# Attention and gated experts on one core: row sums of the probabilities on VectorE, values' products in four array tiles, rounding of the second input on ScalarE and GpSimd

## What is computed

```python
x = x + attn(layernorm(x))         # softmax over 64 keys, then p @ v, then @ Wo.T
p = jax.nn.softmax(scores, axis=-1)
out = jnp.einsum('bhnqk,bhnkd->bhnqd', p, v2)
h = layernorm(x)                    # the second input
y = combine * (silu(h @ w_gate) * (h @ w_up)) @ w_down, summed over experts
x = x + y + shared(h)
```

## Time and profile before

| | |
|---|---|
| median of three runs | 735.25 us (733.56 to 737.29) |
| the profiled execution | 735.13 us, its span 733.3 us |
| TensorE | 690.8 us busy (94%) |
| TensorE weight load | 565.5 us (77%) |
| VectorE | 523.7 us (71%) |
| ScalarE | 532.6 us (73%) |
| GpSimd | 453.3 us (62%) |
| granted TensorE clock | 0.991 of full speed |

### The profile page before, as it was taken

How to read it: one execution, slowest core, us unless ns; L and a number is a source line. 1 busy time by engine, 2 the same in 40 slices (tenths; PEclk the granted TensorE clock), 3 DMA queues, 4 the chain that set the end, 5 groups by cost and what they waited for, 6 DMA issues and landing times.

```text
span 733.3 us, 19496 instructions
## 1 busy us (share of the span) xinstructions
PE 690.8 (94%) x6296; PEld 565.5 (77%) x6296; DVE 523.7 (71%) x1620; ACT 532.6 (73%) x1603; POOL 453.3 (62%) x561
## 2 busy tenths in 40 slices
PE   3899789999999999999999999999999999999997
PEld 2778668787887878788787878788787878778775
DVE  2466676868677786968677786867778686977664
ACT  3686868788787878787787868777787878764332
POOL 6233156767777676767777686777767586445433
PEclk9999999999999999999999999999999999999999
DMA  5010032140413123040314123040313213041321
GB/s 169 1 30 29 2 89 73 37 136 8 131 42 116 57 82 91 24 122 27 119 55 116 57 67 106 11 134 29 116 57 102 71 49 111 4 130 32 116 75 43
DMA packets 50244, 52.59 MB, mean 72 GB/s; under 512 B 5664, under 2 KB 31904, under 8 KB 50080
## 3 DMA queue, kind: packets, MB, share of 16 engines
q1 hardware_dynamic: 50208, 52.14, 23.6%
HBM read 43.20 MB, written 4.72 MB: 65 GB/s over the span
## 4 chain that ended last, share of the span: by engine, by line
PE 65%; POOL 9%; issue 8%; ACT 8%; DVE 8%; DMA 1%; POOLq 0%; SPq 0%; DVEq 0%; ACTq 0%
PE PS L1015 10%; PE PS L822 9%; PE PS L860 9%; PE PS L947 8%; PE PS L824 8%; PE PS L823 8%; ACT probs L581 4%; PE PS L848 3%; POOL X L524 2%; DVE neg_max L738 2%; POOL hh L467 2%; POOL X L518 2%; POOL gate L462 2%; PE PS L1012 2%; PE PS L977 2%
## 5 line engine op out<-in xcount | busy, mean ns | idle before, releaser
L581 ACT ACTIVATE probs<-PS,neg_max 128x96 f32<-128x96 f32 (+1 forms) x1024 | 246.4, 349 | 87.2 <-DVE neg_max L738 87.2
L462 POOL TENSOR_TENSOR gate<-gate,spread 128x512 f32<-128x512 f32 x124 | 158.2, 1276 | 150.8 <-ACT gate L533 86.8
L730 DVE SCALAR_TENSOR_TENSOR tu<-th,PS 128x512 f32<-128x512 f32 x128 | 87.1, 680 | 88.7 <-ACT th L549 75.7
L1015 PE MATMUL PS<-wd,hh 128*128 128x128 f32 x1024 | 136.3, 276 | 4.8 <-DVE hh L791 2.4
L738 DVE TENSOR_REDUCE neg_max<-PS 128x4 f32<-128x384 f32 (+1 forms) x256 | 122.1, 516 | 20.5 <-PE PS L860 17.6
L1015 PEld LDWEIGHTS PS<-wd,hh 128*128 128x128 f32 x1024 | 126.7, 192 | 12.5 <-DVE hh L791 4.9
L467 POOL TENSOR_TENSOR hh<-gate,tu 128x512 f32<-128x512 f32 x100 | 128.2, 1282 | 7.8
L822 PE MATMUL PS<-x_hi,w_hi 128*128 128x512 f32 x288 | 124.6, 433 | 0.2 <-DVE tu L730 0.2
L716 DVE STREAM_TRANSPOSE probsT<-probs 128x768 f32<-128x768 f32 (+1 forms) x128 | 114.6, 895 | 0.0
L824 PE MATMUL PS<-x_lo,w_hi 128*128 128x512 f32 x288 | 114.2, 397 | 0.0
L823 PE MATMUL PS<-x_hi,w_lo 128*128 128x512 f32 x288 | 113.4, 394 | 0.0
(11 more groups left out here) (105 smaller groups left out, 954.4 us busy)
## 6 DMA issues: line engine op xcount, KB each, us to landing
spread<-weights_by_expert SPq DMA_DIRECT2D x248, 128.0 KB, 3.0
X<-x SPq DMA_DIRECT2D x32, 256.0 KB, 3.6
OUT<-H SPq DMA_DIRECT2D x16, 256.0 KB, 3.1
out<-OUT SPq DMA_DIRECT2D x16, 256.0 KB, 2.6
ffn_stage<-w_gu SPq DMA_DIRECT2D x1, 1152.0 KB, 5.6
wd<-w_down SPq DMA_DIRECT2D x1, 512.0 KB, 6.7
weights_by_expert<-cT SPq DMA_DIRECT2D x16, 32.0 KB, 1.6
probsT<-w_att SPq DMA_DIRECT2D x1, 192.0 KB, 3.0
```

The costliest lines, as they stand in the source:

```text
L462: tt(gate2[:, :], gate[:, k % 2, :], spread[:, k % SP_BUFS, :], ALU.mult).then_inc(s_g2, 1)
L581: ins = nc.scalar.activation(probs[:, u % 2, tt, 2 * rows + e, j0:KW], PS[:, rows, n * KW + j0:n * KW + KW], ACT.Exp, bias=neg_max[:, rows ...
L730: v_.scalar_tensor_tensor(tu[:, k % 2, :], th[:, :], 1.0, PS[:, 5, :], ALU.add, ALU.mult).then_inc(s_tu, 1)
L1015: ins = mm(PS[:, 7, r], hh[:, k % 2, r], wd[:, k, :], start=(k == 0 and n == 0), stop=(k == NP - 1), skip_group_check=True)
```

## The change

- The columns of ones go. `v_bd` has 32 columns per block, a product of L947 uses 32 columns of the array, and the four of a block of keys go to four sets of 32 partitions of the same 256 columns.
- VectorE adds up each unit's probabilities (`sum_probs`) into `sums` at the end of the steps that `SUMS` names, one or two units a step, and turns the 32x32 blocks of a sequence into `sums_t` after its fourth unit. In OT, TensorE transposes two halves and spreads `sums_t` over the tokens by four products of 32 columns with columns of the identity.
- `probs` has four buffers; ScalarE waits for the sum of four units ago, in place of the turning of two units ago.
- `x2_hi` is written by ScalarE from PSUM right behind `x2_f`; `x2_lo` by GpSimd at the end of the step, behind LN1. TensorE waits for `second_low_ready` and `second_input_copied` where it waited for the shared bank's semaphores.

```diff
 OE = 13
+SUMS = (11, 12, 13, 13, 14, 14, 15, 16)
 OT, ON, OW = 14, 15, 16
...
+PROB_BUFS = 4
...
 assert len({use[:2] for use in USES}) == len(USES)
-SPLIT = ((LATE, XT), (LATE, XT2), (LATE, XT2 + 4))
+SPLIT = ((LATE, XT),)
...
-ORDER_PER_SLOT = 7
+ORDER_PER_SLOT = 5
...
         v_keys = sb("v_keys", [P, NSB, HG, D])
-        v_bd = sb("v_bd", [P, 2, NSB, HG, 2, 32])
+        v_bd = sb("v_bd", [P, 2, NSB, HG, 32])
         neg_max = sb("neg_max", [P, 2, HG])
-        probs = sb("probs", [P, 2, 2, HG, KW])
+        probs = sb("probs", [P, PROB_BUFS, 2, HG, KW])
         probsT = sb("probsT", [P, 2, HG, NQ, 3, Q])
-        o_f = sb("o_f", [P, 2, T])
+        sums = sb("sums", [P, GB, Q])
+        sums_t = sb("sums_t", [P, GB, Q])
+        o_f = sb("o_f", [P, T])
         o_rs = sb("o_rs", [P, 8, 4])
...
-        headcol = const("headcol")
+        sums_of = ident.rearrange("p (v h c a) -> p c h a v", v=4, h=2, c=4)
...
-        s_ones = sem("ones_beside_values")
...
+        s_x2f = sem("second_input_copied")
+        s_x2l = sem("second_low_ready")
...
+        s_sum = sem("sums_ready")
+        s_sum_t = sem("sums_turned")
...
                         tt(keyrow[:, :], grouprow[:, 0:2], grouprow[:, 2:4], ALU.add).then_inc(s_pool, 1)
-                        for par in range(2):
-                            ones = headcol.unsqueeze(1).broadcast_to([P, NSB * HG, 32])
-                            tt(v_bd[:, par, :, :, 1, :].rearrange("p n g f -> p (n g) f"), ones, ones,
-                               ALU.mult).then_inc(s_ones, 1)
                     g, k = at(sl, s, FF, 1, NP)
...
                            ALU.mult).then_inc(s_xn1, 1)
+                    g, b = at(sl, s, XT2, 4, GB)
+                    if g:
+                        cols = slice(T * b, T * b + T)
+                        taken(pool, sl, s, LATE)
+                        tt(x2_lo[:, g.par, cols], x2_f[:, cols], x2_hi[:, g.par, cols].bitcast(F32),
+                           ALU.subtract).then_inc(s_x2l, 1)
...
                         side, bank = filled(act, sl, s, LATE)
-                        copy(x2_f[:, T * b:T * b + T], bank[:, 0:T]).then_inc(s_high[side], 1)
+                        copy(x2_f[:, T * b:T * b + T], bank[:, 0:T]).then_inc(s_x2f, 1)
+                        copy(x2_hi[:, g.par, T * b:T * b + T], bank[:, 0:T]).then_inc(s_taken[side], 1)
                     def between_halves():
...
                     g, u = at(sl, s, SC, 1, NU)
-                    if g and (u >= 2 or not (g.fixed and g.n == 0)):
-                        act.wait_ge(s_pt, g.n * NU + u - 1)
+                    if g and (u >= PROB_BUFS or not (g.fixed and g.n == 0)):
+                        act.wait_ge(s_sum, g.n * NU + u - PROB_BUFS + 1)
                     for rows in range(2):
...
                                 ins = nc.scalar.activation(
-                                    probs[:, u % 2, tt, 2 * rows + e, j0:KW], PS[:, rows, n * KW + j0:n * KW + KW],
+                                    probs[:, u % PROB_BUFS, tt, 2 * rows + e, j0:KW], PS[:, rows, n * KW + j0:n * KW + KW],
                                     ACT.Exp, bias=neg_max[:, rows, n:n + 1])
...
                         act.wait_ge(s_o_ps, g.n * GB + b + 1)
-                        copy(o_f[:, :, :], PS[:, 2, :].rearrange("p (j q) -> p j q", j=2)).then_inc(s_o, 1)
+                        copy(o_f[:, :], PS[:, 2, 0:T]).then_inc(s_o, 1)
                     g, _ = at(sl, s, XT)
...
                         for v in (2 * half, 2 * half + 1):
-                            ins = copy(v_bd[:, g.par, :, :, 0, D * v:D * v + D].rearrange("p n g d -> p (n g) d"),
+                            ins = copy(v_bd[:, g.par, :, :, D * v:D * v + D].rearrange("p n g d -> p (n g) d"),
                                        v_keys[:, :, :, :].rearrange("p n g d -> p (n g) d"), scale=grouprow[:, v:v + 1])
...
                             v_.transpose(probsT[:, b, :, t0:t0 + 2, c0:3, :].rearrange("p g t c q -> p t g (c q)"),
-                                         probs[:, u % 2, :, :, c0 * Q:KW]).then_inc(s_pt, 1)
+                                         probs[:, u % PROB_BUFS, :, :, c0 * Q:KW]).then_inc(s_pt, 1)
+
+                    def sum_probs():
+                        for u, stage in enumerate(SUMS):
+                            g, _ = at(sl, s, stage)
+                            if not g:
+                                continue
+                            b, t0 = u // 4, 2 * (u % 4)
+                            j0 = Q if u % 4 == 0 else 0
+                            v_.tensor_reduce(sums[:, b, HG * t0:HG * t0 + 2 * HG],
+                                             probs[:, u % PROB_BUFS, :, :, j0:KW].rearrange("p t g k -> p (t g) k"),
+                                             AX_X, ALU.add).then_inc(s_sum, 1)
+                            if u % 4 == 3:
+                                dve.wait_ge(s_sum, g.n * NU + u + 1)
+                                v_.transpose(sums_t[:, b, :], sums[:, b, :]).then_inc(s_sum_t, 1)
...
-                        o_t = bank.rearrange("p (a k v d) -> p a k v d", k=2, v=4, d=D)
-                        link(sl, v_.reciprocal(o_rs[:, :, :], o_t[:, :, 1, :, 0]))
+                        link(sl, v_.reciprocal(o_rs[:, :, :], bank[:, T:T + Q].rearrange("p (a v) -> p a v", v=4)))
                         v_.tensor_tensor(o_n[:, :, :].rearrange("p n (a v d) -> p (n a) v d", v=4, d=D),
-                                         o_t[:, :, 0, :, :],
+                                         bank[:, 0:T].rearrange("p (a v d) -> p a v d", v=4, d=D),
                                          o_rs[:, :, :].unsqueeze(3).broadcast_to([P, 8, 4, D]),
...
                     turn_probs()
-                    g, b = at(sl, s, XT2, 4, GB)
-                    if g:
-                        side, bank = high_out(sl, s, LATE)
-                        cols = slice(T * b, T * b + T)
-                        link(sl, v_.tensor_copy(x2_hi[:, g.par, cols], x2_f[:, cols]))
-                        split_low(x2_lo[:, g.par, cols], x2_f[:, cols], x2_hi[:, g.par, cols]).then_inc(s_taken[side], 1)
                     g, _ = at(sl, s, LN1)
...
                         ins.then_inc(s_taken[side], 1)
+                    sum_probs()
                     g, _ = at(sl, s, XT)
...
                         side, bank = free(EARLY)
-                        use = shared_use(slot_before(sl), (XT2 + 4) % STEPS, LATE)
-                        pe.wait_ge(s_high[use.bank], use.high + 1)
+                        pe.wait_ge(s_x2f, g.n * GB + GB)
                         if g.fixed and g.n == 0:
...
                         if turn_ == 0:
-                            if g.fixed and g.n == 0:
-                                pe.wait_ge(s_ones, 2)
                             pe.wait_ge(s_vb, g.n + 1)
...
                                 pt = probsT[:, b, a, :, :, :].rearrange("p t c q -> p (t c) q")
-                                r0, c0 = 64 * (a % 2), T * (a // 2) + Q * kb
-                                ins = mm(PS[r0:r0 + 64, 2, c0:c0 + Q * nq],
-                                         v_bd[:, g.par, b * NQ + kb, a, :, :].rearrange("p k f -> p (k f)"),
+                                ins = mm(PS[32 * a:32 * a + 32, 2, Q * kb:Q * kb + Q * nq],
+                                         v_bd[:, g.par, b * NQ + kb, a, :],
                                          pt[:, 3 * kb + 2:3 * kb + 2 + 2 * nq - 1:2, :],
-                                         start=(kb == 0 and a < 2), stop=(kb == NQ - 1), skip_group_check=True)
+                                         start=(kb == 0), stop=(kb == NQ - 1), skip_group_check=True)
                         if later:
...
                         pe.wait_ge(s_o, g.n * GB + b + 1)
-                        for n in range(4):
-                            half, j = divmod(n, 2)
-                            ins = nc.tensor.transpose(bank[:, P * n:P * n + P], o_f[:, j, P * half:P * half + P], ident)
+                        for half in range(2):
+                            nc.tensor.transpose(bank[:, P * half:P * half + P], o_f[:, P * half:P * half + P], ident)
+                        pe.wait_ge(s_sum_t, g.n * GB + b + 1)
+                        for c in range(4):
+                            ins = mm(PS[32 * c:32 * c + 32, RING[side], T:T + Q], sums_t[:, b, :], sums_of[:, c, :, :, :],
+                                     start=True, stop=True)
                         ins.then_inc(s_filled[side], 1)
...
                         x2 = x2_hi[:, g.par, :], x2_lo[:, g.par, :]
-                        taken(pe, slot_before(sl), (XT2 + 4) % STEPS, LATE)
+                        pe.wait_ge(s_x2l, g.n * GB + GB)
                         for place, n in ((POST, WG), (LATE, WU)):
```

## The result

The changed kernel takes 729.5 us (median, 729.06 to 729.94) against 737.1 for the kernel before (733.56 to 737.96). The ratio of the fast runs is 0.9928, 95% interval 0.9904 to 0.9951; the two medians alone would give 0.990. The profiled execution took 729.39 us, its span 727.6 against 733.3.

What follows compares the result with a forecast made beforehand. It saw a relay between engines, TensorE only seemingly the bound; 0.1 + 0.6 + 0.2 + 0.3 = 1.2 us a slot over 12.5 slots gives 15, filling some 1: 16 off 735.1, 719 us; forecast 712 to 725, range 706 to 735.

Steps and rivals of the forecast that it cites:

- rival 1: Sums in the way: sums of 1.1 us instead of 0.9 lose some 0.6 a slot on VectorE, 727 us; chance 18%.
- Product stages, -2.5 us of TensorE: TensorE's product stages: four tiles at once instead of two save 2.5 us a slot, at best 2.73, at worst 0.
- Rival 2: Still two tiles at a time: product stages stay at 1.48 and 1.25 us, 734 us likeliest; chance 13%.
- OT stage, +0.1 each: TensorE's OT stage: two transposes go, four tiny products come; +0.1 us a stage, 0.2 a slot.
- Sums, 0.90 and 0.62 us: VectorE's eight sums a slot: 0.90 us for each of 768 elements, 0.62 for each of 512.
- rival 3: Slower: sums blocked by GpSimd, stalling 0.65 us each, five of them without room, 753 us; chance 9%.
- Steps 1 to 3, -0.1: VectorE gets a 0.62 us sum and loses 0.63 of rounding; 0.1 less a slot because the scores come earlier.
- Step 4, -0.6: Normalising chain: statistics of X end 0.62 us further ahead of tu, so GpSimd starts sooner; 0.6 us less.
- Step 5, -0.2: Two sums and a small transpose fit on VectorE, 6.3 us against 6.70; ScalarE's smaller o_f copy saves 0.2.
- Step 6, nothing: VectorE gets sums of 0.62 and 0.90 us, about 4.6 us against 4.85: no change.
- Step 7, -0.3: ScalarE gets some 0.3 us of rounding, TensorE's earlier transposes save most of its 0.54 us wait: net -0.3.
- In the drain about nothing: The draining at the end of the run was forecast to change by about nothing.

Runs made afterwards that it cites:

- e1: Changed kernel with each VectorE sum cut to one key of each row, instructions and waits kept: 728.5 us, ratio 0.9936.
- e11: Changed kernel with the edits of e5, e6 and e7 together and each sum cut to one key: 717.7 us, ratio 0.9756.
- e10: Changed kernel with the four tiles' products issued two tiles at a time, same work: 733.7 us, ratio 0.9959.
- e5: Changed kernel with VectorE's sum into OUT moved from step 5 to the end of step 4: 726.4 us, ratio 0.9859.
- e6: Changed kernel with ScalarE's copy of the second half's high part moved from step 7 into step 0: 728.8 us, ratio 0.9925.
- e7: Changed kernel with the sums ahead of VectorE's wait for GpSimd's gate product in draining slots alone: 728.4 us, ratio 0.9912.
- e15: Changed kernel with 26 tiny writes on VectorE ahead of its first slot, shifting its loop in the program: 729.2 us, ratio 0.9919.
- R: Kernel before with only the second input's rounding moved, high part to ScalarE, low part to GpSimd: 729.1 us, ratio 0.9939.
- P: Products of four tiles; measured with the sums, rounding left on VectorE and the loop shifted (e13): slot 41.32 us against 41.61 before.
- e9: Kernel before with rounding moved, OUT added a step earlier, second half's high part copied a step later: 727.8 us, ratio 0.9888.
- e4: Changed kernel with the rounding back on VectorE, leaving four-tile products and full sums: 746.1 us, ratio 1.0181.
- e13: e4 with 96 tiny writes on VectorE ahead of its first slot, shifting the loop in its program: 735.6 us, ratio 1.0003.

## Why the prediction was right and wrong

The direction was right, the size was not: 16 us forecast, 5 measured. The figure nearest to the measured 729.5 is rival 1's 727, by chance: its mechanism, sums in the way, falls below. Term by term, per slot:

- *Product stages, -2.5 us of TensorE*: right (2.6). Rival 2 falls. By the Trainium skill, "TensorE: Matmul & The Clock Gate", section "Wait — 56ns, not 53.3ns?", starts never come closer than about 25 ns, so that a stage of 32 would by estimate take at least 0.80 us. The trace disagrees for tiles side by side: the records start in fours, 6 to 8 ns apart within a four, and the stage with shorter records took 0.64 us; that the full one took 0.80 is chance. The prediction also reckoned wrongly from that figure: four stages of 0.80 in place of 2 x (1.48 + 1.25) save 2.3 us, 0.2 less than its 2.5 and not 1.1 less, so TensorE would have needed 38.7 us and not 39.6.
- *OT stage, +0.1 each*: 0.60 us for 0.50 at 417.61, and 0.60 for 0.41 at the other, in step 6. About right.
- *Sums, 0.90 and 0.62 us*: 0.92 and 0.65 (mean by shape); a pair of long ones 1.77. Right, and none is held up by GpSimd, so rival 3 falls. By the Trainium skill, "SBUF — State Buffer", section "Who interferes with whom", reductions never do contend with GpSimd, and the trace agrees. Rival 1 falls too: with short sums the slot is the same (e1, e11).
- *Steps 1 to 3, -0.1*: -0.4 (14.58 to 14.15, tu to tu). *Step 4, -0.6*: -0.57 (5.65 to 5.08). *Step 5, -0.2*: -0.21. *Step 6, nothing*: +0.09.
- *Step 7, -0.3: here it failed.* "TensorE's transposes come early enough to save most of the 0.54": they came later in the step than before (1.45 us behind th, 1.21 before), the wait grew to 0.80, and the copy of the high part added 0.26 on top, near the 0.3 that I had for it. From tu to tu the step went from 5.35 to 5.80 us, 0.75 off my figure, and 12.5 slots of that are 9.4 us. By the spans 10.3 us were missed (5.7 for 16). The reason is a wait that my list of waits left out because the change did not add it: TensorE's first down product of step 5 waits for VectorE's OUT. Before, the product stage ahead of it hid that; with the stage 0.6 us shorter it sets the start of everything up to o_n. A shorter product stage ahead of OUT is then worth nothing (e10). OT's extra 0.19 stands behind it with nothing to hide it; what that alone costs no run shows. The prediction also read no row of TensorE behind step 4 (its last is 436.36), so nothing in it placed the transposes of o_n. That the wait for OUT and the copy are the causes, e5 and e6 show: without the one step 7 is 0.41 us shorter, without the other 0.25, and without both it is 5.17.
- *In the drain about nothing*: +3.3 us. I had looked for slack in the loop and assumed the same of the drain, where VectorE has L808 to do. Short sums give 1.2 back (e1). Placing the sums ahead of the wait for GpSimd gives 1.4 (e7), but TensorE's granted clock is low only half as long in that drain as in the changed kernel's; against e15, the changed loop with the clock low as short as in e7, it is 1.0. OUT a step earlier gives 2.8 (e5), with the clock as in e7. The gains overlap. How much of the 3.3 is the clock, and why `spread` takes longer to land, stays open.
- *The sum itself*: steps 1 to 3 gave 4 us more than forecast, step 7 lost 9, step 6 1, the drain 3: together -16 becomes about -6, the difference of the spans.

The parts don't add: R gives 0.57, P 0.29, both 0.68. By the table R shortens steps 1 to 3 by 0.28 and P by 0.34, but both together by 0.35 only; step 4 gives 0.57 with R, nothing with P, 0.67 with both. In step 7 the losses do add, 0.26 and 0.24 to 0.50. With R alone TensorE idles 0.45 us a slot and is the bound (e9); with P alone step 4 stays at 5.68, on the chain of X.

## What to carry to other kernels

When a stage becomes faster, ask what it had hidden: list the waits that stand right behind it, not only those that the change adds. Judge slack stage by stage, in filling and draining too, where a wait for a transfer can take the place of the loop's waits. And when a part of a change costs more than its instructions, look at single iterations instead of their mean: a loss in every loop iteration, at the backward branch, with "issue" as its reason and more packets in the code queue, may be a matter of where the loop lies in that engine's program, and then says nothing about the part. Instructions without effect ahead of the loop test it.

## What the runs showed of the hardware

- A loop's backward branch on VectorE costs 0.3 us or 3.6 to 4.2, by the place of the loop in the program; the long one shows where the engine reaches its branch late (the slot behind it is 1.6 to 2.0 us longer than its neighbour; the loop of e4 takes 11.3 us more than that of e13), and hides where it gets there early (e15).
- Records of products in four tiles of 32 columns come one in 25 and one in 20 ns on average (0.80 and 0.64 us for 32 records), issued two tiles at a time one in 36 and 31 (e10); the order of issue decides, for the same instructions.
- A sum of 768 elements on VectorE is not held up by GpSimd (0.92 us beside it, 0.93 without it), a cast of 256 is (0.9 and 0.25 us, in before).
- The filling takes a different time from kernel to kernel, even where the loops agree to 0.01 us, as TensorE's granted clock drops in it. In e5, with four executions of 720.7 to 727.7 us, the one profiled shows (us, busy of PE, PEld, DVE, ACT, POOL, clock, DMA):

```profile
25.00:50.00 25.00, 20.59 (x189) 16.24 (x188) 17.96 (x39) 15.46 (x55) 10.64 (x7) 0.93 0.08 23
50.00:75.00 25.00, 22.83 (x250) 18.92 (x251) 17.60 (x42) 15.19 (x57) 5.92 (x9) 0.80 0.00 1
75.00:100.00 25.00, 17.59 (x181) 13.51 (x181) 20.92 (x75) 19.36 (x65) 6.51 (x16) 0.85 0.07 22
```

  A mean of 0.80 is a window partly at 1.2 GHz, partly at 2.4; the changed kernel has 0.86, 1.00 and 0.93 there and reaches its first th 6.5 us sooner (99.05 against 105.54). TensorE works with pauses in either (busy 20.6 of the 25 us from 25 to 50 in e5, 20.0 in the changed kernel); what sets off a drop in the one and not in the other no run shows. The drain has such drops too: TensorE is at 1.2 GHz from 640.5 to 647.3 us in the changed kernel, from within its wait for OUT on; in the kernel before the drain has none until the last microseconds (730.3). In this kernel effects of a few us are read from the loop's slots, not from medians.
